# Decoder layer on one core: the key product of the cross-attention whole, and its attended rows divided tile by tile

## The chip, the cores and the metric

One core of a Trainium2 chip runs the kernel. The metric is the device time of one execution in microseconds (us); where several executions were timed, their median. Five engines work side by side, each through its own queue of instructions: PE (TensorE, matrix products), DVE (VectorE), ACT (ScalarE), POOL (GpSimd) and SP, which here only starts transfers. They wait for each other through semaphores.

## What is computed

The inputs are 128 batches of 64 tokens of width 128, float32. A decoder layer with three sublayers, each followed by a layer norm, is applied:

```python
x = _layernorm(x + _L0_attn_ref(x, ...))            # linear attention and a feed-forward part
x = _layernorm(x + _L0_xattn_ref(x, ctx_1024, mask_BxS2_ik0, WQ, WK, WV, WO))
x = _layernorm(x + _L0_ffn_ref(x, ...))             # shared and expert product, gated
```

The change lies in the second line, the cross-attention with 16 heads of width 8:

```python
q = (x @ WQ).reshape(b, s, H, DK).transpose(0, 2, 1, 3)
k = (encoder_output @ WK).reshape(b, s, H, DK).transpose(0, 2, 1, 3)
v = (encoder_output @ WV).reshape(b, s, H, DK).transpose(0, 2, 1, 3)
scores = jnp.einsum('bhqd,bhkd->bhqk', q, k) / SQRT_DK
m = mask[:, None, :, None] + future[None, None, :, :]
scores = jnp.where(m != 0, NEG, scores)
attn = jax.nn.softmax(scores, axis=-1)
ctx = jnp.einsum('bhqk,bhkd->bqhd', attn, v).reshape(b, s, d)
return ctx @ WO
```

## The kernel before

The 8192 tokens are 64 tiles of 128 rows, in 16 groups of four tiles. Three phases follow each other: phase 1 (linear attention), phase 2 (feed-forward part) and phase 3 (cross-attention, third sublayer and the last norm). Phase 3 fills the span from about 250 us on. The change touches phase 3 alone.

Phase 3 is a software pipeline over the groups, `phase3(s, p)` on every engine, written out by hand: step `s` has four slots `t`, one for each tile `n = 4s + t` of group `s`, and between them stands work for its neighbours. The next group `s + 1` gets its queries, keys and values made; the group `s - 1` gets its attended rows turned, multiplied by WO, added and normed; the group `s - 2` goes through the gate and the last norm. Nothing reorders this at run time: an engine takes its instructions in the order of the code, and stands where one waits.

The scores are made for two tiles at once, in the even slots. On PE (line 1525 on) an even slot has

- `scores_open(n + 2, n + 3)` (line 1419): one half of the score products of the next two tiles; it waits until DVE has shifted tile `n + 1` (`sub_ready`) and ACT has copied its probabilities (`pT_ready`);
- `weigh_values(n, t, p)` (line 1449): probabilities times values for tile `n`, into PSUM bank 7. Each head has nine columns, the ninth for the sum of the probabilities;
- `scores_close(n + 2, n + 3)` (line 1430): the other half of the scores. In slot 0 it waits for `opened_maxima` on DVE (`max_ready`).

In slot 0 the key product of the next group, w_xk times cT (128 x 512, into bank 5), is made in two halves of 256 columns by `project_k_half` (line 1487): one between `weigh_values` and `scores_close`, one behind `scores_close`. ACT copies it to k_sb (line 783) when both are done.

On DVE (line 1161 on) `shift` takes the row maxima of a tile's scores and subtracts them (an even tile in two halves, line 1089; an odd one at once, line 1082). Then ACT takes the exponential (line 803), PE turns the probabilities (line 1445), ACT copies them (line 810), and PE weighs the values. `opened_maxima` (line 1056) takes the maxima of the first half of a tile's scores. `residual` (line 1142) adds the product with WO, `rows_product` on PE (line 1242), to X and takes its statistics.

`xattend` (line 1042) divides the weighed values by their sums: a reciprocal (line 1048) and a product (line 1050), out of bank 7 into `att`. Even tiles are weighed into columns 0 to 143 of bank 7 and odd ones into columns 144 to 287, and `xattend` takes two tiles at once: tiles 0 and 1 in slot 1, tiles 2 and 3 in slot 3. So `weigh_values` waits for DVE (`xatt_ready`) in even slots only. In the last step tiles 2 and 3 are divided singly.

Of the kernel before, what the change touches and what calls it, by code (L numbers as in the profile page):

```python
# [52 lines left out]
def decoder_layer(nc, x, ctx, mask, mask_early, ln1_g, ln1_b, wq, wk, wv, wo, ln2_g, ln2_b, w1, w2,  # L53
# [15 lines left out]
    with es:  # L69
# [843 lines left out]
        def _(dve):  # L913
# [128 lines left out]
            def xattend(n, p, part):  # L1042

                dve.wait_ge(pv_done, n + 1)
                count = len(part)
                src = bank(7)[:, H * HV * (part[0] % 2):H * HV * (part[-1] % 2 + 1)] \
                    .rearrange("p (h e) -> p h e", e=HV)
                nc.vector.reciprocal(rec[:, 0, 0:H * count], src[:, :, DH]).then_inc(xrec_ready, count)
                dve.wait_ge(xrec_ready, n + 1)
                nc.vector.tensor_tensor(  # L1050
                    att[p][:, part[0]:part[-1] + 1, :].rearrange("p t (h e) -> p (t h) e", e=DH),
                    src[:, :, 0:DH],
                    rec[:, 0, 0:H * count].unsqueeze(2).broadcast_to([P, H * count, DH]),
                    ALU.mult).then_inc(xatt_ready, count)
# [106 lines left out]
            def phase3(s, p, slots=range(TG)):  # L1161
                prev, old, q = s - 1, s - 2, 1 - p
                for t in slots:
# [3 lines left out]
                    if t == 0 and exists(s):  # L1167
                        opened_maxima(n + 2)
                    if t == 1 and exists(s):
                        shift(n + 1, 0)  # L1170
                    if t == 1 and exists(prev):
                        residual(prev, 6, range(TG))
                    if t == 1 and exists(s):
                        shift(n + 2, 1)
                        after(dve, xatt_xposed, s - 1)
                        xattend(n, p, (0, 1))
# [4 lines left out]
                    if t == 2 and s == LAST:  # L1181
                        xattend(n, p, (2,))
# [4 lines left out]
                    if t == 3 and exists(s):  # L1187
                        xattend(n, p, (3,) if s == LAST else (2, 3))
# [44 lines left out]
        def _(pe):  # L1233
# [215 lines left out]
            def weigh_values(n, t, p):  # L1449

                pe.wait_ge(pT_ready, n + 1)
                if n % 2 == 0 or n == NT - 1:
                    after(pe, xatt_ready, n)
                first = H * HV * (n % 2)
                if n % 2:
                    pe.wait_ge(v4_ready, (n // TG + 1) * QB)
                    pe.wait_ge(future_ready, n // TG + 1)
                    for b in range(QB):
                        nc.tensor.matmul(
                            bank(7)[b * QW:(b + 1) * QW, first:first + H * HV],  # L1460
# [3 lines left out]
                    for i in range(QB):  # L1464
                        for b in range(QB):
                            last = nc.tensor.matmul(
                                bank(7)[b * QW:(b + 1) * QW,
                                        first + QB * HV * i:first + QB * HV * (i + 1)],
# [17 lines left out]

            def project_k_half(q, half):
                cols = slice(GW // 2 * half, GW // 2 * (half + 1))
                return nc.tensor.matmul(bank(5)[:, cols], w_xk[:, :], cT[q][:, cols], start=True, stop=True)
# [35 lines left out]
            def phase3(s, p, slots=range(TG)):  # L1525
                g, q, r = s + 1, 1 - p, s - 1
                for t in slots:
# [34 lines left out]
                    if exists(s):  # L1562
# [4 lines left out]
                        weigh_values(n, t, p)  # L1567
# [96 lines left out]
```

## Time and profile before

| | |
|---|---|
| median of three executions | 550.61 us (549.78 to 551.66) |
| the profiled execution | 552.82 us, its span 551.1 us |
| PE busy | 500.5 us (91%), 9358 matmul records |
| DVE busy | 399.5 us (72%) |
| POOL busy | 373.1 us (68%) |
| ACT busy | 351.3 us (64%) |
| granted TensorE clock, mean | 0.984 of full speed |
| transfers | 17.44 MB, mean 32 GB/s |

The span is the time between the first and the last recorded instruction, and the execution's own time has 1.7 us around it. A float32 product is recorded as two matmuls, one for each of its passes. In a timeline a row is a run of like instructions: its start, the time from its start to the end of its last, the engine, the line and the operation, output and inputs, the count, and in brackets how long the engine had stood idle before and who ended it.

### The profile page before, as it was taken

What the parts mean: (1) busy time and instruction counts of PE and PEld (TensorE: products, weight loads), DVE (VectorE), ACT (ScalarE), POOL (GpSimd) and SP (SyncE); (2) the same over time, 40 slices, a digit from 0 to 9 for tenths busy, and PEclk for the clock granted to TensorE, in tenths of its full rate; (3) what the DMA queues carried; (4) which work ended last, traced back from release to release, by engine and by line L of the source; (5) the groups of instructions that cost most, each with busy time, mean ns of one, the idle gap of its engine ahead of it and who ended that gap; (6) DMA issues with size and microseconds to landing.
All of it is one profiled execution on the core that took longest, in us unless ns stands there. A gap on an engine that the chain in (4) does not pass through costs nothing. (4 is left out here: it accounts for less than half of the span.)

```text
span 551.1 us, 23040 instructions
## 1 busy us (share of the span) xinstructions
PE 500.5 (91%) x9358; PEld 375.0 (68%) x9358; DVE 399.5 (72%) x1356; ACT 351.3 (64%) x637; POOL 373.1 (68%) x684
## 2 busy tenths in 40 slices
PE   3899999998999999999899999989999999999780
PEld 1677777775777777676667776767767677767570
DVE  3777777765677667756568788878778788887866
ACT  2566666656777777764576677757666677766641
POOL 3666666645668774746156878897878778797734
PEclk9999999999999999999899999999999999999977
DMA  6540000000000000010110210221101110110001
GB/s 169 157 133 2 3 2 1 4 2 1 2 0 2 2 1 1 2 30 3 32 32 4 51 44 12 52 51 51 32 24 51 52 39 24 44 51 23 23 2 58
DMA packets 24747, 17.44 MB, mean 32 GB/s; under 512 B 2113, under 2 KB 22465, under 8 KB 24641
## 3 DMA queue, kind: packets, MB, share of 16 engines
q1 hardware_dynamic: 24208, 15.90, 10.6%
q8 instruction: 74, 1.21, 0.9%
q14 instruction: 33, 0.26, 0.2%
q10 hardware_dynamic: 432, 0.07, 0.1%
HBM read 11.77 MB, written 4.19 MB: 29 GB/s over the span
## 5 line engine op out<-in xcount | busy, mean ns | idle before, releaser
L810 ACT ACTIVATE soft<-pair 128x1024 f32<-128x1024 f32 x64 | 51.9, 810 | 50.1 <-PE pair L1445 49.5
L803 ACT ACTIVATE soft<-soft,row_scale 128x512 f32<-128x512 f32 x96 | 66.2, 721 | 15.4 <-DVE soft L1089 10.4
L1387 PEld LDWEIGHTS pair<-w,gel 128*128 128x128 f32 x512 | 60.5, 192 | 8.2 <-issue 5.9
L1387 PE MATMUL pair<-w,gel 128*128 128x128 f32 x512 | 62.7, 276 | 1.0 <-ACT gel L736 1.0
L1348 PE MATMUL pair<-hT,w 128*128 128x512 f32 x128 | 58.3, 595 | 1.3 <-ACT lev L731 1.3
L553 POOL TENSOR_SCALAR k_exp<-k_sb,quad_mask 128x512 f32<-128x512 f32 x64 | 43.2, 693 | 20.1 <-ACT k_sb L783 10.6
L1445 PE MATMUL pair<-ident,soft 128*128 128x128 f32 x384 | 55.6, 281 | 1.3 <-ACT soft L803 1.3
L1076 DVE TENSOR_REDUCE neg_max<-pair 128x16 f32<-128x512 f32 (+1 forms) x48 | 41.1, 856 | 14.5 <-PE pair L1412 14.4
L1445 PEld LDWEIGHTS pair<-ident,soft 128*128 128x128 f32 x384 | 43.3, 141 | 12.0 <-issue 6.4
L515 POOL TENSOR_TENSOR X<-X,proj_sb 128x512 f32<-128x512 f32 x16 | 20.4, 1274 | 35.3 <-ACT proj_sb L694 35.3
L1412 PE MATMUL pair<-k_exp,qT 32*32 32x128 f32 (+1 forms) x2048 | 43.5, 336 | 0.0
L1089 DVE TENSOR_TENSOR soft<-pair,neg_max 128x512 f32<-128x512 f32 x64 | 41.2, 686 | 1.1
L1348 PEld LDWEIGHTS pair<-hT,w 128*128 128x128 f32 x128 | 22.9, 190 | 24.0 <-issue 23.5
L1239 PE MATMUL pair<-ident,xn 128*128 128x128 f32 x192 | 30.6, 283 | 8.6 <-DVE xn L361 8.6
L321 POOL TENSOR_SCALAR veps_b<-mv_b 128x4 f32<-128x4 f32 (+1 forms) x33 | 7.8, 236 | 44.4 <-DVE mv_b L312 25.8
L736 ACT ACTIVATE gel<-lev 128x512 f32<-128x512 int8 x64 | 36.4, 621 | 0.9 <-DVE lev L985 0.9
L1239 PEld LDWEIGHTS pair<-ident,xn 128*128 128x128 f32 x192 | 23.7, 146 | 18.5 <-issue 15.8
L323 POOL TENSOR_TENSOR rstd_b<-veps_b,minus_half 128x4 f32<-128x4 f32 (+1 forms) x33 | 34.4, 1042 | 2.8
L323 POOL TENSOR_TENSOR rstd<-veps,minus_half 128x4 f32<-128x4 f32 x32 | 33.2, 1039 | 2.7
L1476 PEld LDWEIGHTS pair<-v,soft 128*32 128x32 f32 x2048 | 23.6, 109 | 14.7 <-issue 14.7
L1244 PE MATMUL pair<-w_kv,hT 128*128 128x128 f32 x256 | 33.5, 285 | 0.0
L305 DVE BATCH_NORM_STATS2 stats_b<-X 128x6 f32<-128x128 f32 x128 | 28.0, 281 | 5.7 <-DVE X L1146 2.8
(145 smaller groups left out, 1260.1 us busy)
## 6 DMA issues: line engine op xcount, KB each, us to landing
X<-in_x SPq DMA_DIRECT2D x16, 256.0 KB, 3.2
cT<-in_ctx SPq DMA_DIRECT2D x16, 256.0 KB, 3.9
out_rows<-X SPq DMA_DIRECT2D x15, 256.0 KB, 2.6
mask_rows<-in_mask_early SPq DMA_DIRECT2D x16, 128.0 KB, 3.9
w<-in_L_attn_w SPq DMA_DIRECT2D x2, 256.0 KB, 3.3
out_rows<-X SPq DMA_DIRECT2D x2, 128.0 KB, 1.8
w_kv<-in_L_attn_wk SPq DMA_DIRECT2D x1, 64.0 KB, 2.9
w_kv<-in_L_attn_wv SPq DMA_DIRECT2D x1, 64.0 KB, 2.6
```

Source lines behind the costliest of these rows:

```text
L323: nc.gpsimd.tensor_tensor(rstd[:, ts], veps[:, ts], minus_half[:, ts], ALU.pow)\
L553: last = nc.gpsimd.tensor_scalar(k_exp[q][:, h, :], k_sb[:, :], quad_mask[:, h:h + 1], 0.0, ALU.mult, ALU.add)
L736: nc.scalar.activation(gel[:, p, f, :], lev[f][:, :], ACT.Gelu_apprx_tanh, scale=QSTEP).then_inc(gel_ready, 1)
L803: nc.scalar.activation(part, part, ACT.Exp, scale=row_scale[:, n:n + 1])\
L810: nc.scalar.activation(pT[par].rearrange("p (a c) -> p a c", a=2), turned, ACT.Copy)\
L1076: nc.vector.tensor_reduce(neg_max[par][:, :].rearrange("p (a h) -> p a h", a=2), scores, AX.X, ALU.max, negate=True).then_inc(max_ready, 1)
L1089: nc.vector.tensor_tensor(rows[:, heads, :], scores[:, half, :, :], neg_max[par][:, heads].unsqueeze(2).broadcast_to([P, HH, S]), ALU.add) ...
L1239: last = nc.tensor.transpose(dst[:, P * t:P * (t + 1)], src[:, t, :], ident[:, :])
L1348: nc.tensor.matmul(bank(up_bank(s, f)), w_1[:, P * f:P * (f + 1)], hT[p][:, :], start=True, stop=True).then_inc(up_done, 1)
L1387: last = nc.tensor.matmul(bank(6 + q)[:, P * t:P * (t + 1)], gel[:, q, f, P * t:P * (t + 1)], w_2[:, f, :], start=(f == 0), stop=(f == NF ...
L1412: last = nc.tensor.matmul(pair[t % 2][b * QW:(b + 1) * QW, quad // 2, heads], qT[p][rows, batch + first:batch + first + QW], k_exp[p][rows ...
L1445: last = nc.tensor.transpose(dst, probability_rows(n)[:, P * i:P * (i + 1)], ident[:, :])
```

## The change

The key product is made in one piece of 512 columns behind `scores_close` of slot 0. `xattend` takes one tile at a time, in each of the four slots, and all tiles are weighed into columns 0 to 143 of bank 7, so `weigh_values` waits for the tile before it to be divided in every slot. The prologue and the end of the kernel are untouched.

```diff
-            def xattend(n, p, part):
+            def xattend(n, p, t):
                 dve.wait_ge(pv_done, n + 1)
...
-                nc.vector.reciprocal(rec[:, 0, 0:H * count], src[:, :, DH]).then_inc(xrec_ready, count)
+                src = bank(7)[:, 0:H * HV].rearrange("p (h e) -> p h e", e=HV)
+                nc.vector.reciprocal(rec[:, 0, 0:H], src[:, :, DH]).then_inc(xrec_ready, 1)
...
                     if t == 0 and exists(s):
                         opened_maxima(n + 2)
+                        after(dve, xatt_xposed, s - 1)
+                        xattend(n, p, t)
...
                     if t == 1 and exists(s):
                         shift(n + 2, 1)
-                        after(dve, xatt_xposed, s - 1)
-                        xattend(n, p, (0, 1))
+                        xattend(n, p, t)
...
                     if t == 2 and exists(s + 1):
                         future_keys(s + 1, q)
-                    if t == 2 and s == LAST:
-                        xattend(n, p, (2,))
+                    if t == 2 and exists(s):
+                        xattend(n, p, t)
...
                     if t == 3 and exists(s):
-                        xattend(n, p, (3,) if s == LAST else (2, 3))
+                        xattend(n, p, t)
...
             def weigh_values(n, t, p):
                 pe.wait_ge(pT_ready, n + 1)
-                if n % 2 == 0 or n == NT - 1:
-                    after(pe, xatt_ready, n)
-                first = H * HV * (n % 2)
+                after(pe, xatt_ready, n)
...
+                    if exists(s) and t % 2 == 0 and n + 2 < NT:
+                        scores_close(n + 2, n + 3)
                     if t == 0 and exists(g):
                         pe.wait_ge(ctx_loaded[q], (g - q) * 8 + 16)
                         after(pe, moe_ready, s * TG - TG)
                         after(pe, k_ready, g)
-                        project_k_half(q, 0)
-                    if exists(s) and t % 2 == 0 and n + 2 < NT:
-                        scores_close(n + 2, n + 3)
-                    if t == 0 and exists(g):
-                        project_k_half(q, 1).then_inc(xk_done, 1)
+                        project_qk(cT[q], w_xk, bank(5), xk_done)
```

How the instructions stand on PE from the weighing of tile 0 to the turning of tile 1, in a middle step, before:

```order
L1476 MATMUL pair<-v,soft 32x18 [waits xatt_ready,pT_ready,v2_ready]
L1489 MATMUL pair<-cT,w_xk 128x256 [waits k_ready,moe_ready,ctx_loaded1]
L1401 MATMUL pair<-causal_bf,quad_ident 128x256 [waits max_ready,s_opened]
...
L1412 MATMUL pair<-k_exp,qT 32x128 x8
L1489 MATMUL pair<-cT,w_xk 128x256
L1445 MATMUL pair<-ident,soft 128x128 [waits exp_ready]
```

and with the change (the lines of the changed kernel are a few lower):

```order
L1471 MATMUL pair<-v,soft 32x18 [waits xatt_ready,pT_ready,v2_ready]
L1399 MATMUL pair<-causal_bf,quad_ident 128x256 [waits max_ready,s_opened]
...
L1410 MATMUL pair<-k_exp,qT 32x128 x8
L1480 MATMUL pair<-cT,w_xk 128x512 [waits k_ready,moe_ready,ctx_loaded1]
L1443 MATMUL pair<-ident,soft 128x128 [waits exp_ready]
```

The closing scores now follow the weighed values directly, and between them and the turning of tile 1 stand 512 columns of the key product where 256 stood.

On DVE from the shift of tile 3 of a group, in slot 1, to the maxima of the next pair's even tile, in slot 2, before:

```order
L1082 TENSOR_TENSOR soft<-pair,neg_max 128x512 [waits p_xposed,max_ready]
L1048 RECIPROCAL rec<-pair 128x32 [waits pv_done,xatt_xposed]
L1050 TENSOR_TENSOR att<-pair,rec 128x256 [waits xrec_ready]
...
L1157 TENSOR_SCALAR future<-mask_rows,late_key 128x256 [waits pv_done,mask_loaded1,gate_step]
L1076 TENSOR_REDUCE neg_max<-pair 128x16 [waits s_done]
```

and with the change:

```order
L1079 TENSOR_TENSOR soft<-pair,neg_max 128x512 [waits p_xposed,max_ready]
L1046 RECIPROCAL rec<-pair 128x16 [waits pv_done]
L1048 TENSOR_TENSOR att<-pair,rec 128x128 [waits xrec_ready]
...
L1154 TENSOR_SCALAR future<-mask_rows,late_key 128x256 [waits pv_done,mask_loaded1,gate_step]
L1046 RECIPROCAL rec<-pair 128x16 [waits pv_done]
L1048 TENSOR_TENSOR att<-pair,rec 128x128 [waits xrec_ready]
L1073 TENSOR_REDUCE neg_max<-pair 128x16 [waits s_done]
```

The pair of instructions behind the shift has half its columns, and another pair stands ahead of the next maxima.

On DVE around the opened maxima of slot 0, before:

```order
L1059 TENSOR_REDUCE neg_max<-pair 128x2x4 [waits s_opened]
L1072 TENSOR_REDUCE neg_max<-pair 128x2x4 [waits s_done]
L1089 TENSOR_TENSOR soft<-pair,neg_max 128x512 [waits p_xposed,max_ready]
L1089 TENSOR_TENSOR soft<-pair,neg_max 128x512
L1146 TENSOR_TENSOR X<-X,pair 128x512 [waits xproj_done]
```

and with the change:

```order
L1056 TENSOR_REDUCE neg_max<-pair 128x2x4 [waits s_opened]
L1046 RECIPROCAL rec<-pair 128x16 [waits pv_done,xatt_xposed]
L1048 TENSOR_TENSOR att<-pair,rec 128x128 [waits xrec_ready]
L1069 TENSOR_REDUCE neg_max<-pair 128x2x4 [waits s_done]
L1086 TENSOR_TENSOR soft<-pair,neg_max 128x512 [waits p_xposed,max_ready]
```

Tile 0 is now divided between the opened maxima and the maxima of the closed scores.

## Rows read from the trace of the kernel before

**Rows 1.** Busy time by engine and granted clock, middle of phase 3

```profile
280.00:500.00 220.00, 209.75 (x5610) 154.99 (x5580) 174.93 (x543) 152.09 (x280) 172.73 (x303) 1.00 0.15 38
```

**Rows 2.** Waits between 280 and 500 us: total, times, longest

```profile
DVE neg_max L1072 <- PE pair L1412: 17.8, 12, 1.6
...
PE pair L1476 <- issue: 2.7, 4, 0.9
```

**Rows 3.** Timeline of PE, one step, slot 0 to slot 2

```profile
392.23 0.28 PE L1401 MATMUL pair<-causal_bf,quad_ident 32*128 32x256 bf16 x4
...
393.84 0.67 PE L1489 MATMUL pair<-cT,w_xk 128*128 128x256 f32 x2
394.44 0.28 PE L1401 MATMUL pair<-causal_bf,quad_ident 32*128 32x256 bf16 x4
...
395.25 0.70 PE L1489 MATMUL pair<-cT,w_xk 128*128 128x256 f32 x2
395.78 0.60 PE L1445 MATMUL pair<-ident,soft 128*128 128x128 f32 x4
396.22 1.06 PE L1244 MATMUL pair<-w_xo,attT 128*128 128x128 f32 x8
397.11 1.02 PE L1485 MATMUL pair<-yT,w_xq 128*128 128x512 f32 x2
398.07 0.45 PE L1459 MATMUL pair<-v,future 128*32 128x144 f32 x8
...
401.25 0.28 PE L1401 MATMUL pair<-causal_bf,quad_ident 32*128 32x256 bf16 x4 [0.33 <-ACT soft L810]
```

**Rows 4.** Timeline of DVE, the same step

```profile
386.61 1.23 DVE L1076 TENSOR_REDUCE neg_max<-pair 128x16 f32<-128x1024 f32 x1 [0.28 <-PE pair L1412]
...
393.35 0.69 DVE L1059 TENSOR_REDUCE neg_max<-pair 128x8 f32<-128x512 f32 x1 [0.17 <-PE pair L1412]
395.56 0.69 DVE L1072 TENSOR_REDUCE neg_max<-pair 128x8 f32<-128x512 f32 x1 [1.52 <-PE pair L1412]
...
397.49 0.68 DVE L1146 TENSOR_TENSOR X<-X,pair 128x512 f32<-128x512 f32 x1
...
400.46 0.69 DVE L1082 TENSOR_TENSOR soft<-pair,neg_max 128x512 f32<-128x512 f32 x1
```

**Rows 5.** Timeline of ACT, the same step, the copy of tile 2's probabilities

```profile
399.88 1.02 ACT L810 ACTIVATE soft<-pair 128x1024 f32<-128x1024 f32 x1 [1.05 <-PE pair L1445]
```

**Rows 6.** Timeline of PE, slot 0 of the last step

```profile
514.91 0.28 PE L1401 MATMUL pair<-causal_bf,quad_ident 32*128 32x256 bf16 x4 [0.24 <-ACT soft L810]
...
516.92 0.28 PE L1401 MATMUL pair<-causal_bf,quad_ident 32*128 32x256 bf16 x4 [0.39 <-DVE neg_max L1059]
```

**Rows 7.** Timeline of DVE, slot 0 of the last step

```profile
516.09 0.68 DVE L1059 TENSOR_REDUCE neg_max<-pair 128x8 f32<-128x512 f32 x1
```

**Rows 8.** Timeline of PE, slot 1 of the step at 340 us

```profile
343.74 1.06 PE L1244 MATMUL pair<-w_xo,attT 128*128 128x128 f32 x8
```

**Rows 9.** Timeline of DVE, the same slot

```profile
344.84 0.69 DVE L1146 TENSOR_TENSOR X<-X,pair 128x512 f32<-128x512 f32 x1
```

**Rows 10.** Groups of instructions by line and shape: busy, mean ns

```profile
L1050 DVE TENSOR_TENSOR att<-pair,rec 128x256 f32<-128x256 f32 x31 | 13.2, 425 | 3.6 <-DVE rec L1048 0.5
...
L1048 DVE RECIPROCAL rec<-pair 128x32 f32<-128x32 f32 x31 | 10.8, 348 | 0.0
...
L1050 DVE TENSOR_TENSOR att<-pair,rec 128x128 f32<-128x128 f32 x2 | 0.6, 292 | 0.1
L1048 DVE RECIPROCAL rec<-pair 128x16 f32<-128x16 f32 x2 | 0.5, 258 | 1.2 <-PE pair L1476 0.8 <-PE pair L1466 0.4
```

**Rows 11.** Timeline of PE, slot 2 of the first step

```profile
260.08 1.15 PE L1500 MATMUL pair<-w_xv,cT 128*64 128x64 f32 x32
261.27 0.28 PE L1401 MATMUL pair<-causal_bf,quad_ident 32*128 32x256 bf16 x4
```

**Rows 12.** Busy time by engine and granted clock, behind the first step

```profile
268.00:270.00 2.00, 2.00 (x14) 1.63 (x12) 0.60 (x1) 1.55 (x3) 0.00 (x0) 0.50 0.00 0
```

More of the change, by code:

```diff
@@ L1040, in phase2 @@
                                   ln_a.offs, r * 2)
-            def xattend(n, p, part):
+            def xattend(n, p, t):
                 dve.wait_ge(pv_done, n + 1)
-                count = len(part)
-                src = bank(7)[:, H * HV * (part[0] % 2):H * HV * (part[-1] % 2 + 1)] \
-                    .rearrange("p (h e) -> p h e", e=HV)
-                nc.vector.reciprocal(rec[:, 0, 0:H * count], src[:, :, DH]).then_inc(xrec_ready, count)
+                src = bank(7)[:, 0:H * HV].rearrange("p (h e) -> p h e", e=HV)
+                nc.vector.reciprocal(rec[:, 0, 0:H], src[:, :, DH]).then_inc(xrec_ready, 1)
                 dve.wait_ge(xrec_ready, n + 1)
[L1050 to L1054, printed above, removed]
+                nc.vector.tensor_tensor(att[p][:, t, :].rearrange("p (h e) -> p h e", e=DH),
+                                        src[:, :, 0:DH],
+                                        rec[:, 0, 0:H].unsqueeze(2).broadcast_to([P, H, DH]),
+                                        ALU.mult).then_inc(xatt_ready, 1)
             def opened_maxima(n):
@@ L1459, in weigh_values @@
                         nc.tensor.matmul(
-                            bank(7)[b * QW:(b + 1) * QW, first:first + H * HV],
+                            bank(7)[b * QW:(b + 1) * QW, 0:H * HV],
                             future[p][:, t // 2, b * QW:(b + 1) * QW],
@@ L1466, in weigh_values @@
                             last = nc.tensor.matmul(
-                                bank(7)[b * QW:(b + 1) * QW,
-                                        first + QB * HV * i:first + QB * HV * (i + 1)],
+                                bank(7)[b * QW:(b + 1) * QW, QB * HV * i:QB * HV * (i + 1)],
                                 pT[1][:, P * i + b * QW:P * i + (b + 1) * QW],
@@ L1485, in project_qk @@
                 nc.tensor.matmul(dst, w[:, :], src[:, :], start=True, stop=True).then_inc(done, 1)
-            def project_k_half(q, half):
-                cols = slice(GW // 2 * half, GW // 2 * (half + 1))
-                return nc.tensor.matmul(bank(5)[:, cols], w_xk[:, :], cT[q][:, cols], start=True, stop=True)
             def turn_y(g):
```

## The prediction

> **What bounds the kernel now.** I read the busy shares by stretch first: in the middle of phase 3 PE is busy 209.75 of 220 us at full clock, DVE 174.93, ACT 152.09 and POOL 172.73 [rows 1]. So PE is near its limit, yet not quite the whole bound. The list of waits then tells who waits for whom: DVE stands 1.5 us in each step for the closing scores of slot 0, 17.8 us over 12 steps [rows 2]. Last I took one step apart in the timelines. A wait of PE recurs at 401.25, where the opening scores of slot 2 start 0.33 us after PE was free [rows 3]. The releaser named is ACT's copy, but that ended at 399.88 + 1.02 = 400.90 [rows 5]; DVE's shift ended at 400.46 + 0.69 = 401.15 [rows 4], 0.10 before. So DVE ends that wait. DVE's chain starts at the closing scores of slot 0 (394.44, DVE at 395.56) and runs almost without a gap up to that shift [rows 3, 4]. The loop that sets a step is therefore: opening scores of slot 2, then PE's queue to the closing scores of slot 0, then DVE's queue back to the opening scores of slot 2. The change touches the end of the PE part and the start of the DVE part.
>
> **Closing scores of slot 0 (moved ahead).** Before, 0.60 us of the key product stood ahead of them (393.84 to 394.44) [rows 3]. Now they follow the weighed values and could start at about 393.8, but they need the opened maxima, and these run from 393.35 to 394.04 [rows 4]. They cannot run sooner, since they wait for the opening scores, which stand as they did (392.23). The last step has no key product and shows the new arrangement already: the maxima end at 516.09 + 0.68 = 516.77 and the closing scores start at 516.92, after 0.39 us of idle PE [rows 6, 7]. So 0.15 us lie between the two, and I put the start at 394.04 + 0.15 = 394.19, 0.25 us earlier than before. Of the 0.60 us of product taken out of the way, 0.35 us turn into a new wait of PE.
>
> **Key product in one piece.** The second half took 395.25 to 395.78, 0.53 us; the first 0.60 [rows 3]. The whole product of the same form (queries, 128x512) takes 397.11 to 398.07, 0.96 us [rows 3]. So the pieces cost 1.13 us and the whole 0.96, a saving of 0.17 us that I take in full, since it is the same shape and line of code. Behind the closing scores PE is now occupied 0.96 where it was 0.53: 0.43 us more. With the 0.25 earlier start, everything on PE from the turning of tile 1 on comes 0.43 - 0.25 = 0.18 us later (395.78 becomes 395.96).
>
> **What DVE makes of it.** DVE's maxima and shift of tile 2 start 0.25 us earlier. Behind them stands the residual, which needs PE's product with WO. That product ended at 396.22 + 1.06 = 397.28 and the residual started at 397.49, so it had not been waiting [rows 3, 4]. How soon it can start is seen at 344.84, where the product had ended at 343.74 + 1.06 = 344.80: 0.04 us [rows 8, 9]. With the change the product ends at 397.46 and the residual can start at 397.50. DVE would have been ready at 397.24, so it now waits 0.26 us there, and the residual starts at 397.50 against 397.49: **0.01 us later**. From there to the opening scores of slot 2 DVE's queue is the same. PE's side of that point: it was free 0.33 us ahead, now 0.15; the copy of tile 2's probabilities ends 0.18 later, at 401.08. Both still come before DVE's 401.16. The gain at the closing scores is thus given back at the residual: 0.01 us in each of 12 steps, 0.1 us.
>
> **Where that cover is missing.** Fourteen steps have a key product and a residual; I found two (the one at 344.84 is one) in which the residual already waited for PE. There PE's 0.18 us count in full: 0.36. The first step has no residual, and its opening scores follow the value product without idle (260.08 + 1.15 against 261.27) [rows 11]: 0.18. In the last step the opened maxima started behind DVE's own queue, about 0.07 us after the scores would have let them; DVE is lighter ahead of them now: -0.07.
>
> **Attended rows tile by tile.** Two instructions on two tiles took 348 + 425 ns, on one tile 258 + 292 [rows 10]. DVE gains 0.22 us at each of the two old places (slots 1 and 3) and pays a pair of 0.55 us and about 0.10 between the two instructions, 0.65 us, at each new one. Over 16 steps DVE is busy some 10 us longer. Slot 0: the pair stands between the opened maxima (end 394.04) and the maxima of the closed scores, which come at 395.31; 1.27 us of waiting hide 0.65. Were that cover gone, its whole 0.65 us would be in the loop. Slot 2: DVE had 0.28 us idle ahead of 386.61 and comes 0.22 earlier, 0.50 us against 0.65: the shift of tile 0 of the next group starts up to 0.15 late. The pair of slot 3 is 0.22 shorter, which makes this good before the opened maxima, where 0.17 us of idle stood as well [rows 4]. Cost nothing. The weighing in odd slots now waits for the division of the tile before; that is over by about 394.7 for tile 1, weighed at 398.07 [rows 3], and likewise in slot 3. Queued behind these waits is all of PE's work, but they are met more than 0.9 us early. Cost nothing. No transfer is added or moved; ACT's copy of the keys comes 0.18 later and POOL, whose spreading of them follows, has idle time before its next norm.
>
> **Sum:** 0.12 + 0.36 + 0.18 - 0.07 = +0.6 us. On the profiled execution that is 552.82 + 0.6 = 553.4 us; the median shown is 2.2 us below that execution, so I forecast 550.61 + 0.6 = **551.2 us**. The bounds of the unknown costs: the gap of 0.15 us between maxima and closing scores could be 0.10, as from DVE to PE at 401.25, or 0.20; each 0.05 gives 0.05 us in a step, 0.75 us in all. This case by itself runs from 550.0 to 552.3. A measurement of this kernel can tell about 0.3%, 1.65 us, from no change.
>
> **Rivals.**
>
> *Late maxima (slower).* If DVE reaches the opened maxima so late that the closing scores start no sooner than before (394.44), PE is 0.43 us late behind the key product, and the residual starts at 397.28 + 0.43 + 0.04 = 397.75, 0.26 late. Fourteen steps and the first: 14 x 0.26 + 0.43 = 4.1 us, **554.7 us**. It begins to decide when DVE's new pair in slot 2 costs over about 0.25 us more than the 0.65 I worked out, since so much is in reserve (0.17 idle and what the shorter pairs leave over). For it speaks that DVE carries 10 us more and its reserve is thin; against it that the parts of the pair are measured. 0.17.
>
> *The whole product saves nothing (slower).* If in its new place it costs the 1.13 us of its halves, PE is 0.35 late and the residual 0.18: 14 x 0.18 + 0.35 = 2.9 us, **553.5 us**. The Trainium skill (TensorE: Matmul & The Clock Gate, Back-to-back issue gap) says as much: a warm matmul's gap is its columns over 2.4 GHz plus a fixed 2.5 ns, so that joining two halves would save 2.5 ns for each pass. The trace disagrees with this by its 0.60 and 0.53 against 0.96 [rows 3]. 0.06.
>
> *Less lateness on PE (faster side).* If the residual can start as early as its queue allows, DVE's 0.25 us stay, cut off by PE's 401.10 and the copy's 401.08: about 0.12 us in 12 steps, less 0.5: -0.9 us, **549.7 us**, and 548.8 if the closing scores also follow the maxima sooner. Against it: the residual's wait for PE is plain in the code. 0.10, of which 0.04 beyond 0.3%.
>
> *PE's stray stalls.* PE stood four times within the weighing of tile 2, 2.7 us in all, for nothing that the profile shows [rows 2], and behind the first step the clock was granted at half for a stretch [rows 12], which is 1.2 of 2.4 GHz, after idle time of PE. A program with 30 fewer key matmuls and a new wait of 0.35 us in each step may move either. All the stalls gone gives **548.5 us**, as many again or another half-clock stretch 553 to 554. 0.17: 0.08 faster, 0.03 same, 0.06 slower. That the change does nothing is not a rival, since the order of instructions shows it.
>
> **How the numbers follow.** My forecast has 0.50: 0.45 within 0.3%, 0.05 above. Faster is 0.04 + 0.08 = 0.12; slower 0.05 + 0.17 + 0.06 + 0.06 = 0.34; the same 0.45 + 0.06 + 0.03 = 0.54. The range of 8 in 10 reaches down to near the first stray stalls gone, 549.0, and up to just short of the late maxima in full, 554.5.
>
> **What would show it.** PE idle ahead of the closing scores of slot 0, released by the opened maxima, about 0.35 us in 15 steps; the whole key product at 0.96 us; the residual now waiting for the product with WO, about 0.26 us, where no such wait is listed; DVE's wait ahead of the maxima of slot 2 gone; the opening scores of slot 2 still 0.10 us behind DVE's shift, and a step without stalls as long as before. The prediction is wrong if these opening scores follow PE's own work or the copy, if PE waits in the weighing of an odd tile, or if the opened maxima have no idle DVE ahead of them.

## The result, and the profile after

The changed kernel took **548.66 us** (median of 12 executions, 546.45 to 550.62) and the kernel before, timed beside it, 551.38 us (12 executions, 548.91 to 552.75). The ratio is 0.995 with a 95% interval of 0.9928 to 0.9972: 2.7 us faster. The forecast was 0.6 us slower, and the measured time lies just below its range. The profiled execution of the changed kernel took 548.83 us with a span of 547.1, 4.0 less than the span of before; its mean granted clock is 0.989 where before had 0.984.

The busy line of the page, whole span:

```profile
PE 496.1 (91%) x9328; PEld 369.3 (67%) x9328; DVE 407.1 (74%) x1418; ACT 349.7 (64%) x637; POOL 371.9 (68%) x684
```

DVE is busy 7.6 us longer, where the forecast had some 10; PE has 30 matmul records less. The middle of phase 3 by stretch (start and end; length, then busy time and count of PE, PEld, DVE, ACT and POOL; granted clock, share of DMA, GB/s), to be held against [rows 1]:

```profile
280.00:500.00 220.00, 209.65 (x5549) 152.66 (x5538) 181.61 (x595) 150.06 (x278) 173.38 (x306) 0.99 0.15 38
```

DVE has 6.7 us more work in it and PE the same. The waits of that stretch (engine and line, who is waited for; total, times, longest):

```profile
DVE neg_max L1069 <- PE pair L1410: 9.6, 13, 0.7
...
PE pair L1399 <- DVE neg_max L1056: 4.3, 13, 0.3
...
DVE X L1143 <- PE pair L1242: 2.0, 12, 0.2
...
PE pair L1399 <- issue: 0.9, 1, 0.9
PE pair L1410 <- issue: 0.2, 1, 0.2
```

Three lines are the forecast mechanism: DVE waits less for the closed scores of slot 0 (9.6 us where [rows 2] have 17.8), PE waits for the opened maxima, and the residual waits for the product with WO. The last two lines are stalls that the profile gives no cause for: 1.1 us, where before had 2.7 in the weighing [rows 2] and 0.5 more elsewhere. The timelines of one step, first PE, which answers to [rows 3]:

```profile
392.00 0.28 PE L1399 MATMUL pair<-causal_bf,quad_ident 32*128 32x256 bf16 x4
...
393.95 0.28 PE L1399 MATMUL pair<-causal_bf,quad_ident 32*128 32x256 bf16 x4 [0.33 <-DVE neg_max L1056]
...
394.75 1.13 PE L1480 MATMUL pair<-cT,w_xk 128*128 128x512 f32 x2
395.72 0.60 PE L1443 MATMUL pair<-ident,soft 128*128 128x128 f32 x4
...
401.02 0.28 PE L1399 MATMUL pair<-causal_bf,quad_ident 32*128 32x256 bf16 x4 [0.16 <-ACT soft L810]
```

and DVE, which answers to [rows 4]:

```profile
386.56 1.23 DVE L1073 TENSOR_REDUCE neg_max<-pair 128x16 f32<-128x1024 f32 x1 [0.23 <-PE pair L1410]
...
393.11 0.69 DVE L1056 TENSOR_REDUCE neg_max<-pair 128x8 f32<-128x512 f32 x1
393.75 0.26 DVE L1046 RECIPROCAL rec<-pair 128x16 f32<-128x16 f32 x1
394.04 0.29 DVE L1048 TENSOR_TENSOR att<-pair,rec 128x128 f32<-128x128 f32 x1
395.06 0.69 DVE L1069 TENSOR_REDUCE neg_max<-pair 128x8 f32<-128x512 f32 x1 [0.73 <-PE pair L1410]
...
397.25 0.69 DVE L1143 TENSOR_TENSOR X<-X,pair 128x512 f32<-128x512 f32 x1 [0.17 <-PE pair L1242]
```

From the opening scores of slot 0 to the closing ones PE now takes 393.95 - 392.00 = 1.95 us, where before took 394.44 - 392.23 = 2.21 in this step; from there to the opening scores of slot 2 it takes 7.07 where it took 6.81. The 0.26 us won at the first place are lost at the second, at the residual. So a step without stalls is as long as before.

The 4.0 us of span came from elsewhere. First, the middle of phase 3, from the first step's opening scores of slot 2 to those of the step before the last, went from 245.7 us (261.27 [rows 11] to 506.94) to 243.8 (261.42 to 505.20). Either execution has one stretch of 3.4 us at half clock in it, the kernel before behind the first step [rows 12] and the changed one near 368 us, behind a stall. The changed kernel at these two places:

```profile
268.00:270.00 2.00, 1.76 (x46) 1.10 (x43) 0.45 (x1) 1.84 (x3) 0.00 (x0) 1.00 0.00 0
...
367.00:369.00 2.00, 1.85 (x36) 0.95 (x36) 0.38 (x1) 0.00 (x0) 1.92 (x2) 0.59 0.03 8
```

The first two steps are 1.2 us shorter for it and the step at 355 us 1.3 us longer, so the clock cancels here. The 1.9 us are waits of PE in the other steps, of which the changed kernel has fewer and shorter ones.

Second, the end. In the last step PE waits for the attended rows of that step's own tiles 0 and 1; here is what follows that wait in the timeline of PE, before:

```profile
524.48 0.69 PE L1521 MATMUL pair<-ident,att 128*128 128x128 f32 x2 [2.95 <-DVE att L1050]
...
533.74 0.38 PE L1239 MATMUL pair<-ident,xn 128*128 128x128 f32 x2
```

and after:

```profile
522.37 0.44 PE L1512 MATMUL pair<-ident,att 128*128 128x128 f32 x2 [2.64 <-DVE att L1048]
...
529.45 0.38 PE L1237 MATMUL pair<-ident,xn 128*128 128x128 f32 x2
```

The same work took 9.26 us before and 7.08 after, 2.18 less. The granted clock tells why: 0.50 of full speed (1.2 of 2.4 GHz) from 524 to 528 us before, full speed after. First the kernel before, then the changed one:

```profile
524.00:528.00 4.00, 3.52 (x75) 3.15 (x76) 1.92 (x9) 1.37 (x3) 1.79 (x5) 0.50 0.00 0
```

```profile
524.00:528.00 4.00, 3.90 (x62) 3.30 (x61) 2.82 (x12) 2.17 (x5) 1.57 (x5) 1.00 0.02 4
```

These are two executions. Whether such differences belong to the kernels or to the draw is what the experiments had to settle.

### The profile page after: what moved, and what is told of

It reads as the page before. It is cut to its first block and busy times, and to the rows that moved or that the text cites. A ratio compares the mean times of both kernels' runs of the same rounds, so it can differ in the third digit from the quotient of the medians.

```text
span 547.1 us, 23025 instructions
## 1 busy us (share of the span) xinstructions
PE 496.1 (91%) x9328; PEld 369.3 (67%) x9328; DVE 407.1 (74%) x1418; ACT 349.7 (64%) x637; POOL 371.9 (68%) x684
## 5 line engine op out<-in xcount | busy, mean ns | idle before, releaser
L1410 PE MATMUL pair<-k_exp,qT 32*32 32x128 f32 (+1 forms) x2048 | 44.6, 336 | 0.2 <-issue 0.2
L1242 PEld LDWEIGHTS pair<-w_kv,hT 128*128 128x128 f32 x256 | 31.0, 198 | 1.2
```

Source lines behind the costliest of these rows:

```text
L1242: last = nc.tensor.matmul(dst[:, P * t:P * (t + 1)], src[:, P * t:P * (t + 1)], w, start=True, stop=True)
L1410: last = nc.tensor.matmul(pair[t % 2][b * QW:(b + 1) * QW, quad // 2, heads], qT[p][rows, batch + first:batch + first + QW], k_exp[p][rows ...
```

## The experiments

Times are medians; each ratio is to the kernel before in the same batch, with its 95% interval. Three explanations were possible: the key product costs or gains, the attended rows gain in the middle, the last step gains through idle time and clock. (The letters of the theories in the boxes are those of each box.)

### The two halves of the change apart

`e1_k_whole`: the pairs of before, the key product in one piece.

```diff
-                        project_k_half(q, 0)
                     if exists(s) and t % 2 == 0 and n + 2 < NT:
                         scores_close(n + 2, n + 3)
...
-                        project_k_half(q, 1).then_inc(xk_done, 1)
+                        project_qk(cT[q], w_xk, bank(5), xk_done)
```

> Only the key product is moved and made whole; the rows are divided in pairs as before. My theory A (the clean step did not change; what was won is full clock and fewer stalls on PE): closing scores of slot 0 1.95 to 2.02 us behind the opening ones (2.18 before), 7.07 from there to the opening scores of slot 2 (6.81 before), a step without stalls 17.1 us, the time within 1 us of the kernel before. Rival B (the move of the key product is what won 2.7 us): 548.7, 2 to 3 us below the kernel before. Rival C (DVE is late with its pairs, so the maxima come late): closing scores at 2.02, step 17.2, time 1 to 2 us above.

Measured 554.52 us against 551.95, ratio 1.0036 (1.0011 to 1.0061): slower.

`e2_att_tiles`: the other half alone, `xattend(n, p, t)` in every slot, with the key product in its two pieces.

> Only the rows are divided tile by tile; the key product is in two halves as before. Theory A with its tail (the division behind the shift of the last step is 0.2 to 0.3 us shorter, PE stands 2.64 instead of 2.95 us before it turns the attended rows, and the stretch at half clock behind that wait comes less often): the time 1 to 2.7 us below the kernel before, a clean step 17.1, idle time before the turning in the last step 2.6 to 2.7. Rival B (the key product won it): time within 1 us of the kernel before.

Measured 550.83, ratio 0.997 (0.9951 to 0.9989): faster.

`e3_last_tiles`: tiles 0 and 1 divided singly in the last step only.

```diff
+                    if t == 0 and s == LAST:
+                        after(dve, xatt_xposed, s - 1)
+                        xattend(n, p, (0,))
...
-                        xattend(n, p, (0, 1))
+                        xattend(n, p, (1,) if s == LAST else (0, 1))
...
```

> Only in the last step are tiles 0 and 1 divided singly; all other steps and the key product are as before. If the tail is what won (theory A with its tail), this alone gives most of the 2.7 us: 1 to 2.7 us below the kernel before, with PE idle 2.6 to 2.8 us before it turns the attended rows and the granted clock mean higher by 0.002 to 0.005. If the gain lies in the steps, it gives 0.3 us at most.

Measured 552.09, ratio 0.9996 (0.9975 to 1.0016): nothing. PE's wait there is 2.64 us, as in the changed kernel, and the clock still fell to half in its profile. The shorter wait of the last step alone is not what gains.

`e4_before_fill`: the kernel before, with work for PE in the last step's wait.

```diff
                     if t == 2 and s == LAST:
+                        for _ in range(12):
+                            nc.tensor.transpose(bank(4)[:, 0:P], ident[:, :], ident[:, :])
                         pe.wait_ge(xatt_ready, n)
```

> The kernel before, with 12 more transposes of the identity into a free bank in the last step, ahead of PE's wait for the attended rows (2.95 us idle). They change no result. If a stretch at half clock behind that idle time costs the kernel before some 2 us, the fill takes it away: 2 us below the kernel before, granted clock 1.00 from 523 to 530 us. If the half clock there is rare or costs nothing, the time stays within 0.5 us; if the fill delays the turning, it is up to 1 us above.

Measured 550.4, ratio 0.9982 (0.9961 to 1.0004): 1.5 us less, at the edge of what can be told. Its twelve executions fall in two groups: four with a mean clock of 0.981 to 0.987 took 552.8 to 553.1 us, eight with 0.989 to 0.993 took 549.3 to 550.9. Its profiled execution is one of the four and still has half clock from 527.1 to 530.5 us. The changed kernel's twelve do likewise: four at 0.986 to 0.987 took 549.9 to 550.6 us, eight at 0.989 to 0.992 took 546.5 to 549.6. A stretch at half clock more or less is worth 1 to 2 us, and an execution draws them.

So the gain sits in the attended rows, and the key product seemed to cost 2.6 us that no step without stalls shows. In the step before the last of `e1_k_whole`, in the closing scores of slot 2, stands a stall that of all the versions only `e7_k_whole_quiet` below has too, with the same order of PE's work and 0.95 us long:

```profile
509.31 0.43 PE L1412 MATMUL pair<-k_exp,qT 32*32 32x128 f32 x10 [1.45 <-issue]
```

### Where PE's stray stalls come from

Counting PE's records (matmuls, weight loads, semaphore instructions), every stall of 0.2 us or more in phase 3, in all twenty traces, stands where that count is 191 or 192 modulo 256. (In phase 1 the trace has thirteen gaps of 0.39 us without a releaser, one in each 6.7 us and the same in all versions; they stand at no such count, and what they are is open.) The page lists the transfers that bring instructions as a queue of its own; in the profile of `e13_att_tiles_fill`:

```profile
q8 instruction: 74, 1.21, 0.9%
```

74 packets of 16384 bytes, where PE has 19113 records, 74 times 256 and a rest. In time order, a packet starts around each such crossing, from 1.2 us before it to 2.7 us behind it, and every stall ends 1.2 to 1.6 us after a packet's end. From the trace's records (us of the span; the block is the time from one crossing to the next):

```
kernel               crossing  packet starts  ends    next crossing  block
before               364.23    366.05         367.02  368.23 (stall)  4.00
before               399.78    401.16         402.14  403.51 (stall)  3.73
e13_att_tiles_fill   397.97    400.19         401.18  402.43 (stall)  4.46
e18_odd_wait_dve     469.99    472.39         473.36  474.85 (stall)  4.87
e15 (no loads)       432.59    433.18         434.44  436.54          3.96
e16 (no loads)       431.23    431.93         433.13  435.18          3.94
```

The stall of the first line in the timeline of PE, kernel before:

```profile
366.81 0.48 PE L1476 MATMUL pair<-v,soft 128*32 128x18 f32 x31
368.23 0.24 PE L1476 MATMUL pair<-v,soft 128*32 128x18 f32 x4 [0.94 <-issue]
```

So PE waited for its own instructions. The packet of one crossing is needed at the next, and PE stands still where it gets through a block before the packet has started, has run (0.9 to 1.8 us) and 1.2 to 1.6 us more have passed. So the start decides: with a packet 1.82 us behind its crossing the block of the first line took 4.00 us, stall included, while from 305.42 to 308.46 us of the same trace, with the packet 0.6 us behind, a block of 3.0 us passed without a stall. In the kernel before 29 of the 52 blocks from 255 to 520 us take 5 us or more; in all twenty traces only one such block ends in a stall, of 5.1 us in `e17_odd_wait_fill` below. The Trainium skill (Runtime: NRT & Kernel Launch, Instruction fetch mechanics) gives a store of two lines of 16 KiB filled in sequence, with 128 KiB for PE named beside it, and refills of 256 instructions. The packet size and the count of 256 agree; that a late packet is missed at the very next crossing fits the two lines and not the 128 KiB. It also says that the fetch is hidden because instructions are issued more slowly than it fills; the 0.94 us above disagree.

Two things follow, and were tried. The transfers of the kernel's own data may hold the packet back; and a change that adds or drops PE instructions moves the crossings. A step has 896 records before (3.5 blocks), 894 after, 892 in `e1_k_whole`, 898 in `e2_att_tiles`.

**Without the loads** of encoder output and mask (four versions, with the edit below; the results are still stored, and the output is another):

```diff
-                if exists(s + 2):
-                    if s >= 0:
-                        sp.wait_ge(future_ready, s + 1)
-                        load_mask(s + 2, p)
-                    after(sp, xv_done, s + 1)
-                    load_ctx(s + 2, p)
+                if s == -1:
+                    load_ctx(1, 1)
...
-                dve.wait_ge(mask_loaded[q], g // 2 * 16 + 16)
+                dve.wait_ge(mask_loaded[q], 16)
...
-                        pe.wait_ge(ctx_loaded[q], (g - q) * 8 + 16)
+                        pe.wait_ge(ctx_loaded[q], 16)
```

> The kernel before without the loads of contexts and masks for groups 2 to 15 (the first two groups' are used again, the output of the later groups is another; no other work is left out). Theory D: PE's stray stalls stand where it reaches a new block of its instructions (every 256th instruction in the traces so far) while a load of 256 KB is on its way, and they are what the change moved. Then these stalls (0.2 to 1.1 us in 9 of 13 steps, 4.9 us) shrink to under 0.3 us each, the time is 3 to 6 us below the kernel before, and the four kernels without loads differ by what the clean step says. Rival: the stalls do not hang on the loads; then the time stays within 1 us of the kernel before.

> The changed kernel without the same loads. Theory D: against the kernel before without loads (e5) it is level, within 1 us, since a step without stalls differs by 0.03 us only (17.12 against 17.09). Rival E (the change wins in the work itself, not in stalls): it is 2 to 3 us below e5.

> The whole key product alone, without the same loads. Theory D: within 1 us of e5 (a clean step 17.13). Rival F (the 1.8 us that it lost are in its own steps, where tile pairs and the wait for the maxima meet): 1.5 to 2.5 us above e5.

> The rows divided tile by tile alone, without the same loads. Theory D: within 1 us of e5, a few tenths below for the end. Rival G (the divisions win 1.4 us in DVE's queue): 1 to 2 us below e5.

Against 551.12 for the kernel before: `e5_before_quiet` 547.74, `e6_after_quiet` 548.03, `e7_k_whole_quiet` 551.0 and `e8_att_tiles_quiet` 545.72 (ratios 0.9948, 0.9949, 0.9997 and 0.992, each within 0.003). The stalls in the weighing of tile 2 are gone: all that PE's list of waits from 280 to 500 us has left of stalls in `e5_before_quiet`, in the weighing of an odd tile, is

```profile
PE pair L1462 <- issue: 0.5, 2, 0.3
```

In the table above the packet starts 1.4 to 2.4 us behind the crossing in the first four lines and 0.6 to 0.7 in the last two: at these places the loads hold it back, and leaving them out is worth 3.4 us to the kernel before. They are not needed for a late packet, though: the one before the stall of 0.95 us in `e7_k_whole_quiet` starts 1.54 us behind its crossing. Before and after are level here: without the loads the whole change gains nothing. But `e7_k_whole_quiet` is still 3.3 us over the kernel before treated the same, and `e8_att_tiles_quiet` 2.0 under it, so the loads alone don't explain the halves. In the profiled executions the second of these is the last step: from its opening scores on `e5_before_quiet` takes 36.1 us, with half clock from 518.8 to 525.7, and `e8_att_tiles_quiet` 34.0, at full clock there. That is why the end is taken away from both sides further down.

**With equal counts of records.** Increments of a semaphore on PE that nobody waits for bring a version to another's count:

```diff
                         project_qk(cT[q], w_xk, bank(5), xk_done)
+                        for _ in range(4):
+                            pe.sem_inc(pad_step)
```

> The whole key product alone (e1), and behind it in each step four increments of an unused semaphore on PE, so that PE's instructions count the same in each step as in the kernel before (896 instead of 892 by the records) and every 256th stands again where it stood. Theory H: what e1 lost is the place at which PE reaches a new block of 256 instructions (in e1 a wait of 0.95 to 1.45 us within the closing scores of slot 2 of the last step, none there before). Then that wait is gone, the stalls stand in the weighing of tile 2 as before, and the time is level with the kernel before or up to 0.6 us above. Rival: e1's loss is in the product's place; then it stays 1.5 to 3 us above.

> The changed kernel with two such increments in each step (896 instead of 894 by the records: the blocks of the kernel before). Theory H: the 2.7 us that the change won are gone for the most part, the time 0 to 1 us below the kernel before, with stalls of 0.6 to 1.1 us in the weighing of tile 2 in every other step. Rival: the change won them in its own work; then it stays 2 to 3 us below.

> The kernel before with two such increments in each step (898 instead of 896, as in the kernel with the rows divided singly, e2). Nothing else is changed. Theory H: level with e2, so 0.5 to 1.5 us below the kernel before, with the places of the stalls moving by some matmuls from step to step as in e2. Rival: nothing changes, within 0.5 us of the kernel before.

`e9_k_whole_pad4` (896) took 552.07 against 551.54, ratio 1.0001 (0.9985 to 1.0017): the whole key product is worth nothing at the count of before, and the stall of 1.45 us in the step before the last is gone. So the key product neither costs nor gains; that `e1_k_whole` was slow by the place of its crossings is likely, but the intervals of 1.0036 and 1.0001 just overlap. `e10_after_pad2` (896) took 550.07, ratio 0.9968 (0.9951 to 0.9985); `e11_before_pad2` (898) 552.76, ratio 1.0013 (0.9997 to 1.0029). At equal counts the tile-by-tile rows gain 2.0 us (550.07 against 552.07) and 2.4 (0.997 against 1.0013, in two batches). Perhaps 1 us of the changed kernel's 2.7 is its count of 894 (0.995 against 0.9968); the intervals overlap, so this part is not shown.

### By what path the tile-by-tile rows gain

`e12_after_fill`: the changed kernel with the twelve transposes of `e4_before_fill`.

> The changed kernel with the 12 more transposes in the last step's wait, as in e4. If the half clock behind that wait costs about 3 us when it falls there, and the fill makes it rarer, the time is 1 to 2 us below the changed kernel, so 3.7 to 4.7 us below the kernel before; the rival is that the changed kernel has hardly any such stretch left: within 0.5 us of it.

Measured **547.15** against 551.54, ratio 0.9911 (0.9891 to 0.993): the fastest version with the right output, 1.5 us under the changed kernel, 2.1 by the ratios (0.9911 against 0.995), whose intervals touch. The idle time ahead of the last step's turning is halved, and what follows runs at full clock:

```profile
518.03 1.47 PE L1544 MATMUL pair<-ident 128*128 128x128 f32 x12
520.83 0.44 PE L1512 MATMUL pair<-ident,att 128*128 128x128 f32 x2 [1.33 <-DVE att L1048]
```

Four runs took the end away from both sides by this fill, two of them the loads as well; all have 898 records in a step. Against the same two versions without the fill it gave 0.26 and 0.27% again (`e13_att_tiles_fill` 0.9944 where `e2_att_tiles` had 0.997, `e14_before_pad2_fill` 0.9986 where `e11_before_pad2` had 1.0013).

> The attended rows tile by tile with the key product in halves, plus twelve transposes of the identity ahead of the last step's wait for the attended rows. PE has 898 instruction records in a step, as in the kernel that it is compared with, the kernel before with two increments and the same fill. Theory F (the gain of about 2.2 us is mostly in the clock granted at the end): the two stand within 0.6 us, both near 550 to 551. Theory S (it is in stalls of PE in the middle of phase 3): the gap stays at about 2 us, this kernel near 549, the other near 551. Theory W (work of the last step alone): a gap of 0.3 us.

> The kernel before with two increments of a semaphore on PE per step and the twelve transposes. Theory F: near 550.5, since the version without the fill took 552.8 and the fill gave 1.5 us elsewhere, and level with the tile-by-tile kernel with the fill. Theory S: near 551.3, some 2 us over it, with stalls in slot 0's closing scores (0.3 to 0.6 us) and in the weighing of tile 2 (0.5 to 0.8 us) in its timeline that the other lacks or has shorter. Theory W: 0.3 us over it.

> The kernel before with two increments per step, the twelve transposes, and without the transfers of the encoder output and of the mask for groups 2 and later (those groups compute with the data of group 0 or 1, so the output is not the reference's). Stalls and the clock at the end are taken away as far as I know how. All theories: near 546.5, as the kernel without these transfers took 547.7 and the fill gave about 1.5. Theories F and S: within 0.5 us of the tile-by-tile kernel treated the same. If the division tile by tile gains by its work, it stays some 2 us behind it.

> The attended rows tile by tile with the key product in halves, with the twelve transposes and without the transfers of the encoder output and of the mask for groups 2 and later (those groups compute with the data of group 0 or 1). It took 545.7 without the fill, where its profile had no stretch at half clock behind the last step's wait. Theories F and S: 545 to 546, within 0.5 us of the kernel before treated the same. If the gain is in the work itself: 2 us less than that one.

Measured 548.89 (`e13_att_tiles_fill`, ratio 0.9944, 0.9921 to 0.9968) against 550.57 (`e14_before_pad2_fill`, 0.9986, 0.9968 to 1.0005), and 545.95 (`e16_att_tiles_quiet_fill`, 0.9894, 0.9868 to 0.9921) against 547.57 (`e15_before_quiet_pad2_fill`, 0.992, 0.9896 to 0.9945). The gap stays at 1.7 and 1.6 us: it is not the clock at the end, and not the loads. Nor is it the clock elsewhere, although the profiled executions of `e14_before_pad2_fill` and `e15_before_quiet_pad2_fill` have a stretch at half clock behind the first step that their partners lack: the executions with a mean clock of 0.991 or more alone have medians of 548.75 against 550.30 us, and 545.88 against 547.49. Theory S, which the first pair bears out, had expected no gap in the second. The lists of waits of PE from 280 to 500 us show stalls in all four. `e13_att_tiles_fill`:

```profile
PE pair L1471 <- issue: 1.5, 3, 0.6
PE pair L1410 <- issue: 0.2, 1, 0.2
```

`e14_before_pad2_fill`:

```profile
PE pair L1477 <- issue: 2.3, 3, 1.1
PE pair L1413 <- issue: 1.1, 3, 0.7
```

`e15_before_quiet_pad2_fill`:

```profile
PE pair L1409 <- issue: 1.5, 3, 0.7
```

`e16_att_tiles_quiet_fill`:

```profile
PE pair L1406 <- issue: 0.5, 1, 0.5
```

They stand at the same places of the program in each pair, and are shorter or missing where the rows are divided tile by tile: 1.7 against 3.4 us, 0.5 against 1.5. The other pairs of equal count agree: 1.0 (`e10_after_pad2`) against 2.7 (`e9_k_whole_pad4`), 2.3 (`e2_att_tiles`) against 2.8 (`e11_before_pad2`).

The last two runs asked whether that belongs to the division or to the queues. Both have PE's queue as `e13_att_tiles_fill` has it, but for one record that is missing at the very first odd tile (19112 against 19113), with the division in pairs. The second was to have the length of its DVE queue too. By the traces it overshoots: DVE has 1935 records in `e13_att_tiles_fill`, 1921 in `e17_odd_wait_fill` and 2045 in `e18_odd_wait_dve_fill`, because most of the added single divisions need no record of their own for their waits. So the two runs stand on either side of it, one record a step short and seven over.

```diff
-                if n % 2 == 0 or n == NT - 1:
-                    after(pe, xatt_ready, n)
+                after(pe, xatt_ready, n if n % 2 == 0 or n == NT - 1 else n - 1)
...
                     if t == 0 and exists(s):
                         opened_maxima(n + 2)
+                        for _ in range(4):
+                            dve.sem_inc(pad_dve)
...
+                    elif t == 2 and exists(s):
+                        for _ in range(4):
+                            dve.sem_inc(pad_dve)
```

> The kernel before with the twelve transposes and, ahead of the weighing of each odd tile, a wait of PE for a division long past. Its PE queue is that of the tile-by-tile kernel with the fill, instruction for instruction; the division on DVE is two tiles at once as before. Theory Q (the gain lies in PE's queue, the place of its instructions in the blocks that are fetched): near 549.0, as that kernel. Theory D (it lies on DVE's side, in the division or in the instructions added): near 550.6, as the kernel before with two increments and the fill.

> The same, with four increments of a semaphore on DVE behind the opened maxima of slot 0 and four behind the mask work of slot 2, so that DVE's queue too is as long as in the tile-by-tile kernel. Theory Q: as the run beside it, near 549. Theory D by the length of DVE's queue: near 549, with the run beside it near 550.6. Theory D by the division itself (rows of one tile are ready earlier, the pairs are shorter): 550.6 like the run beside it; the increments may cost up to 0.2 us of DVE in a step, which idle time hides.

Measured 552.61 (ratio 1.0022, 1.0003 to 1.004) and 552.0 (1.0005, 0.9987 to 1.0024), where `e13_att_tiles_fill` had 0.9944 to its own neighbour. So PE's queue does not explain the gain, and the length of DVE's does not as far as a shorter and a longer one tell: with PE's queue the same, dividing tile by tile is worth about 0.6%, 3.4 us against the second run. What still differs with the division is the place of DVE's instructions in its queue and the columns of bank 7; no run takes these apart. In the list of waits of `e18_odd_wait_dve_fill`:

```profile
PE pair L1481 <- issue: 2.6, 4, 0.8
PE pair L1471 <- issue: 0.6, 2, 0.4
PE pair L1418 <- issue: 0.3, 1, 0.3
```

3.5 us (4.9 in `e17_odd_wait_fill`), against 1.7. That both runs came out above `e14_before_pad2_fill`, which differs in where two records of a step stand, shows how much such a place can matter (ratios 1.0022 and 0.9986, intervals that touch by 0.0002).

**What is shown and what stays open.** Shown: the gain hangs on the division tile by tile; it remains at equal counts, there also without the loads and with the clock at the end held up, and with PE's queue the same. In every pair of equal count the profiled execution has less time of PE waiting for instructions, though one execution each is a thin basis: the 0.5 to 1.8 us between such sums are of the size of the gain, not a proof of it. One execution can even point the other way: `e1_k_whole` has 0.4 us of stalls from 280 to 500 us and 1.45 behind, less than the 3.2 of the kernel before, and a median 2.6 us above it. Not shown: the share of the count of 894 in the changed kernel's time. Open: by what path a division that comes one slot earlier makes these waits shorter. A step without stalls is equally long in both forms (17.09 to 17.10 us in `e2_att_tiles` and in the kernel before). That the earlier division keeps the queues of PE and DVE further from each other's limits when a packet is late, so that a stall is made up for rather than passed on, is a guess that no run tests.

## Why the prediction was wrong

- **Closing scores of slot 0: right.** Forecast 0.25 us earlier and 0.35 of new waiting; measured 0.26 and 0.33, in 13 steps.
- **Key product in one piece: right.** Forecast 0.96 us; from 394.75 to 395.72 it is 0.97. That the whole product would save nothing, one of the rivals, is refuted in the rows.
- **The gain is given back at the residual: right.** The wait that was not there before is 0.17 us instead of 0.26, and the step without stalls 0.03 us longer instead of 0.01. `e9_k_whole_pad4` confirms it as a time: 1.0001.
- **Attended rows, their cost to the loop: right in mechanism.** The pair of slot 0 is hidden (DVE still idles 0.73 us behind it). The pair of slot 2 costs less than the 0.65 I took: DVE still had 0.23 us of idle ahead of the maxima at 386.56, where I expected them up to 0.15 late. That this wait would be gone was one of my signs, and it did not come true. DVE is busy 7.6 us longer in all, where I had some 10.
- **"Cost nothing" for the attended rows: the step that failed.** I costed the division by the path of a step without stalls, where it is indeed nothing, and put the whole of it at zero. At equal counts of PE records it gained 1.6 to 2.4 us in four pairs, and 3.4 in the fifth, with PE's queue the same. The term should have been about -2. By what path is open; in each of these pairs PE waits less for instructions in the profiled execution, and such waits were in none of my terms for the division.
- **"PE's stray stalls": named, but given too little.** I held them for chance and gave 0.08 to the faster side, with 548.5 us if all of them went. Their places are no chance: they stand at multiples of 256 records of PE's queue, the loads lengthen them, and a change of PE's count of instructions moves them. The change's two records fewer in a step may have given 1 us more. With -2 and -1 my sum of +0.6 would have been -2.4, where -2.7 was measured; the second of these terms is not clear of noise.
- The rivals on the slow side did not occur: the opened maxima are not late, and the whole product saves what its rows said.

## What to carry to other kernels

When a profile shows short waits of PE for nothing, count its instructions: if they recur at a fixed number, as here at every 256th record, look whether the packets of the instruction queue come late there. What stands around such a point can then be worth as much as a change of the loop: leaving out the loads gained 3.4 us here (no run only moved one), and two to four records more in a step went with -2.4 to +1.2 us. For the same reason compare two versions of a kernel at equal counts of instructions before a difference of half a per cent is put down to the edit. And a loop worked out from a step without stalls gives a bound, not the time: here it was right to 0.02 us a step and still missed the sign.

## What the runs showed that I had not expected

- PE stood still for 0.2 to 1.45 us where the 16384-byte packet with its next instructions came late, and each such wait ended 1.2 to 1.6 us after the packet's end. With the kernel's own loads the packet started 1.4 to 2.4 us behind the crossing in the dense blocks of the table, without them 0.6 to 0.7.
- Four semaphore increments in a step, which do nothing, moved `e1_k_whole` from 554.52 to 552.07 us (ratios 1.0036 and 1.0001, intervals just overlapping).
- Twelve transposes thrown away in a wait of 2.64 us made the changed kernel 1.5 us faster; in the profiled execution the engine was granted full clock behind it. Of the eight profiled executions with this fill seven have no stretch at half clock between 515 and 532 us, of the twelve without it two.
